# Two-layer fp32 kernel: one h-tile split moved ahead of a Gelu, row transposes grouped in twos, and a reordered tail

## What is computed

```python
# layer 0: an MLP, whose last 128 output columns use an expert chosen per batch
h = gelu(x @ fc1_w.T + fc1_b)                     # 512 -> 2048
x = x + concat(h @ fc2_w.T + fc2_b,               # 2048 -> 384
               h @ experts_w[e].T + experts_b[e]) # 2048 -> 128
# layer 1: masked pooling
s = tanh(x @ W1 + b1) @ v                         # one score for each token
p = softmax(where(mask, s, -1e30))                # mask: l <= j, l >= j or l != j, by batch
x = x + (p @ x) / count_of_mask
```

## Time and profile before

| | us |
|---|---|
| median of 3 runs | 774.71 |
| lowest and highest | 774.32 and 776.2 |
| the profiled execution's own time | 774.91 |
| its span, first to last instruction | 773.1 |
| PE busy in the span | 760.9 |

### The profile page before, as it was taken

The page is one execution under the profiler, slowest core; times in us unless marked ns, Lnnn a source line. Parts: engine busy times, 40 slices in busy tenths (PEclk is TensorE's granted clock), DMA queues, the critical chain, the costliest instruction groups (busy, mean ns, idle before and its releaser), DMA issues.

```text
span 773.1 us, 11505 instructions
## 1 busy us (share of the span) xinstructions
PE 760.9 (98%) x3465; PEld 621.8 (80%) x3465; DVE 403.2 (52%) x701; ACT 387.4 (50%) x669; POOL 131.8 (17%) x199
## 2 busy tenths in 40 slices
PE   8999999999999999999999999999999999999996
PEld 6788888888888888888888888888888888888875
DVE  6955666573445332754545433286355533246767
ACT  6856665453546533544446633445354662344543
POOL 3273230400011121320001022040000102204001
PEclk9999999999999999999999999999999999999998
DMA  6999997877874558877776566886787566697732
GB/s 218 297 338 325 311 348 260 273 227 234 246 205 150 177 190 285 261 218 234 214 231 207 150 202 214 277 257 180 244 260 205 171 189 205 214 287 216 212 113 109
DMA packets 130715, 176.93 MB, mean 229 GB/s; under 512 B 10064, under 2 KB 97632, under 8 KB 130656
## 3 DMA queue, kind: packets, MB, share of 16 engines
q1 hardware_dynamic: 130496, 176.20, 72.7%
q0 software_dynamic: 160, 0.01, 0.1%
HBM read 136.33 MB, written 39.85 MB: 228 GB/s over the span
## 4 chain that ended last, share of the span: by engine, by line
PE 93%; DVE 3%; ACT 1%; DMA 1%; issue 1%; SPq 0%; DVEq 0%
PE y L778 15%; PE y L780 15%; PE y L779 15%; PE hA L778 7%; PE hA L779 7%; PE hA L780 7%; PE hF L778 5%; PE hF L780 5%; PE hF L779 5%; PE j L871 2%; PE j L848 1%; PE j L850 1%; PE j L847 1%; PE j L778 1%; PE j L779 1%; PE j L780 1%
## 5 line engine op out<-in xcount | busy, mean ns | idle before, releaser
L778 PE MATMUL y<-hs,w2c 128*128 128x512 f32 x512 | 201.9, 394 | 0.6 <-DMA w2c<-exs 0.4
L780 PE MATMUL y<-hs,w2c 128*128 128x512 f32 x512 | 199.6, 390 | 0.0
L779 PE MATMUL y<-hs,w2c 128*128 128x512 f32 x512 | 199.3, 389 | 0.0
L778 PEld LDWEIGHTS y<-hs,w2c 128*128 128x128 f32 x512 | 96.1, 188 | 22.8 <-DVE hs L1300 1.9
L780 PEld LDWEIGHTS y<-hs,w2c 128*128 128x128 f32 x512 | 96.1, 188 | 20.5
L779 PEld LDWEIGHTS y<-hs,w2c 128*128 128x128 f32 x512 | 96.2, 188 | 19.3
L778 PE MATMUL hA<-xch,w1c 128*128 128x512 f32 x252 | 99.4, 394 | 2.2 <-DVE xcl L1300 1.7
L780 PE MATMUL hA<-xch,w1c 128*128 128x512 f32 x252 | 98.2, 390 | 0.0
L779 PE MATMUL hA<-xcl,w1c 128*128 128x512 f32 x252 | 98.2, 390 | 0.0
L1048 ACT ACTIVATE hst<-hst,bcol 128x512 f32<-128x512 f32 x62 | 43.9, 721 | 85.2 <-DVE hst L1500 85.2
L1300 DVE TENSOR_TENSOR hs<-gb,hs 128x512 fp32r<-128x512 f32 x64 | 43.5, 716 | 64.4 <-ACT hs L994 64.4
(11 more groups left out here) (284 smaller groups left out, 1110.2 us busy)
## 6 DMA issues: line engine op xcount, KB each, us to landing
w2c<-w2s SPq DMA_DIRECT2D x114, 384.0 KB, 3.6
w1c<-w1s SPq DMA_DIRECT2D x24, 768.0 KB, 4.6
w2c<-exs SPq DMA_DIRECT2D x114, 128.0 KB, 4.0
w1c<-w1s SPq DMA_DIRECT2D x48, 256.0 KB, 3.8
w1c<-w1s SPq DMA_DIRECT2D x24, 512.0 KB, 4.0
x1T<-in_x SPq DMA_DIRECT2D x32, 256.0 KB, 5.8
w1s<-w1c SPq DMA_DIRECT2D x8, 768.0 KB, 4.1
w2s<-w2c SPq DMA_DIRECT2D x16, 384.0 KB, 4.3
```

Of the source, the lines that this page charges most:

```text
L778: nc.tensor.matmul(ps, ah, bh, start=first, stop=False, skip_group_check=onto)
L779: nc.tensor.matmul(ps, ah, bl, start=False, stop=False, skip_group_check=onto)
L780: return nc.tensor.matmul(ps, al, bh, start=False, stop=last, skip_group_check=onto)
```

## The change

There are four edits.

1. In the last pair of a batch, ACT makes the high part of h tile 14 before it waits for the second Gelu (order 4) and not after it.
2. In the stages, the row transposes `xn` 0 and 1 both follow unit 21 (u = 7), and `xn` 2 and 3 both follow u = 9. Before they stood at u = 7, 8, 9 and 10. The difference `xs` 5 moves from u = 9 to u = 10.
3. In the tail, the 8 pieces of units 30 and 31 come in the order of `LAST_UNITS`: two pieces of unit 30 come before the first of unit 31.
4. In the tail, the scans, the exponentials (now `expG` for two of them and `expO` for the other two), `total`, `den` and `rd` come earlier. `own_chunk` 0 to 3 stand ahead of `rd`, and 4 to 7 in one block behind the first four `pool`. Low part 1 of W stands on DVE behind `pool` 3.

```diff
-          6: [("attn",)], 7: [("xn", 0)], 8: [("xn", 1)], 9: [("xn", 2)], 10: [("xn", 3)], 11: [("score",)]}
+          6: [("attn",)], 7: [("xn", 0), ("xn", 1)], 9: [("xn", 2), ("xn", 3)], 11: [("score",)]}
...
+LAST_UNITS = [(-2, 0), (-2, 1), (-1, 0), (-1, 1), (-2, 2), (-1, 2), (-2, 3), (-1, 3)]
...
-    ("expPW", 0), ("sums",), ("scan",), ("expPW", 1), ("total",)] + [("pool", c) for c in range(BC)] + [
-    ("den",), ("rd", 0, CH)] + [("pool", c) for c in range(BC, CH)]
-
-OWN_BEFORE = {("total",): range(BC), ("pool", 0): [4], ("rd", 0, CH): [5], ("pool", 6): [6], ("pool", 7): [7]}
+    ("expPW", 0), ("scan",), ("sums",), ("total",), ("expPW", 1), ("den",), ("rd", 0, CH)] + [("pool", c) for c in range(CH)]
+
+OWN_BEFORE = {("rd", 0, CH): range(BC), ("pool", BC): range(BC, CH)}
...
-    ("full", 2), ("expP", 0), ("expW", 0), ("hiP", 0), ("hiW", 0), ("full", 3), ("expP", 1), ("hiP", 1), ("sums",), ("expM",),
-    ("expW", 1), ("hiW", 1)]
+    ("full", 2), ("expG",), ("expP", 0), ("hiP", 0), ("expW", 0), ("hiW", 0), ("full", 3), ("expO",), ("sums",),
+    ("expP", 1), ("hiP", 1), ("expW", 1), ("hiW", 1)]
...
-FULL_BEFORE = {("bc", 0): 1, ("bc", 1): 2, ("total",): 4}
+FULL_BEFORE = {("bc", 0): 1, ("bc", 1): 2, ("total",): 3, ("rd", 0, CH): 4}
...
-                gate(pool, den_exp, b * NEXP + (6 - NEXP))
+                gate(pool, den_exp, b * NEXP + (5 - NEXP))
                 gate(pool, den_scan, b * NSCAN + (2 - NSCAN))
                 nc.gpsimd.tensor_tensor(short_of(FG), short_of(FG), short_of(FS), ALU.mult).then_inc(den_in, 1)
                 gate(pool, den_in, b * NIN + (5 - NIN))
+                gate(pool, den_exp, b * NEXP + (6 - NEXP))
...
-                    for oc in range(OC):
-                        for n in (-2, -1):
-                            fc2(kind, b, n, oc)
+                    for n, oc in LAST_UNITS:
+                        fc2(kind, b, n, oc)
...
                 gelu(b, p, 3)
+                if p == PAIRS - 1:
+
+                    split_h(b, 2 * p)
                 gelu(b, p, 4)
...
-                split_h(b, 2 * p)
+                if p < PAIRS - 1:
+                    split_h(b, 2 * p)
                 split_h(b, 2 * p + 1)
```

More of the change, by code:

```diff
@@ L86 @@
 POST_U = {1: [("ysum", oc) for oc in range(OC)], 2: [("x1", 0)], 3: [("x1", 1)], 4: [("x1", 2)], 5: [("x1", 3)],
[L87 removed]
+          6: [("attn",)], 7: [("xn", 0), ("xn", 1)], 9: [("xn", 2), ("xn", 3)], 11: [("score",)]}
 PREP_U = {0: [("xc", 0), ("xs", 0)], 2: [("xc", 1), ("xs", 1)], 3: [("xc", 2)], 4: [("xc", 3), ("xs", 2)],
[L90 to L91 removed]
+          5: [("xc", 4), ("xc", 5)], 6: [("xs", 3)], 7: [("xc", 6)], 8: [("xc", 7), ("xs", 4)], 9: [("xc", 8)],
+          10: [("xc", 9), ("xs", 5)], 11: [("xc", 10), ("xs", 6)], 12: [("xc", 11), ("xc", 12)], 13: [("xs", 7)], 14: [("xc", 13)]}
 EX_P = [(0, 1), (1, 0), (1, 2), (2, 1)]
@@ L97 @@
 X_LOADS = {5: ((0, 1), 3, 2), 7: ((3,), 4, 3), 8: ((2,), 6, 3)}
+LAST_UNITS = [(-2, 0), (-2, 1), (-1, 0), (-1, 1), (-2, 2), (-1, 2), (-2, 3), (-1, 3)]
 TAIL_ORDER = [("ysum", oc) for oc in range(OC)] + [("x1", oc) for oc in range(OC)] + [
     ("xn", 0), ("xn", 1), ("attn",), ("xn", 2), ("xn", 3), ("score",), ("stats",), ("expE",), ("mT",), ("bc", 0), ("bc", 1),
-    ("expPW", 0), ("sums",), ("scan",), ("expPW", 1), ("total",)] + [("pool", c) for c in range(BC)] + [
-    ("den",), ("rd", 0, CH)] + [("pool", c) for c in range(BC, CH)]
-OWN_BEFORE = {("total",): range(BC), ("pool", 0): [4], ("rd", 0, CH): [5], ("pool", 6): [6], ("pool", 7): [7]}
+    ("expPW", 0), ("scan",), ("sums",), ("total",), ("expPW", 1), ("den",), ("rd", 0, CH)] + [("pool", c) for c in range(CH)]
+OWN_BEFORE = {("rd", 0, CH): range(BC), ("pool", BC): range(BC, CH)}
 TAIL_ACT = [("x1", oc) for oc in range(OC)] + [
     ("xn", 0), ("xn", 1), ("attn",), ("xn", 2), ("xn", 3), ("full", 0), ("full", 1), ("expE",), ("expS",), ("expF",), ("expD",),
-    ("full", 2), ("expP", 0), ("expW", 0), ("hiP", 0), ("hiW", 0), ("full", 3), ("expP", 1), ("hiP", 1), ("sums",), ("expM",),
-    ("expW", 1), ("hiW", 1)]
+    ("full", 2), ("expG",), ("expP", 0), ("hiP", 0), ("expW", 0), ("hiW", 0), ("full", 3), ("expO",), ("sums",),
+    ("expP", 1), ("hiP", 1), ("expW", 1), ("hiW", 1)]
 TAIL_DVE = [("ysum", 0), ("ysum", 1), ("x1", 0), ("ysum", 2), ("x1", 1), ("ysum", 3), ("x1", 2), ("x1", 3), ("xn", 0),
-            ("xn", 1), ("score",), ("stats",), ("mT",), ("xn", 2), ("expE",), ("bc", 0), ("xn", 3), ("bc", 1), ("loP", 0), ("loW", 0),
-            ("scan",), ("loP", 1), ("sums",), ("total",), ("loW", 1), ("den",), ("rd", 0, CH)] + [("pool", c) for c in range(CH)]
-FULL_BEFORE = {("bc", 0): 1, ("bc", 1): 2, ("total",): 4}
+            ("xn", 1), ("score",), ("stats",), ("mT",), ("xn", 2), ("expE",), ("bc", 0), ("xn", 3), ("scan",), ("loP", 0), ("loW", 0),
+            ("bc", 1), ("total",), ("sums",), ("den",), ("loP", 1), ("rd", 0, CH)] + [("pool", c) for c in range(BC)] + [
+            ("loW", 1)] + [("pool", c) for c in range(BC, CH)]
+FULL_BEFORE = {("bc", 0): 1, ("bc", 1): 2, ("total",): 3, ("rd", 0, CH): 4}
 def body(kind):
@@ L1136, in task_part @@
                 elif task[0] == "expM":
-                    exps_M(b)
+                    exp_runs(b)
+                    exp_own(b)
+                elif task[0] == "expG":
+                    exp_runs(b)
+                elif task[0] == "expO":
+                    exp_own(b)
                 elif task[0] == "expPW":
@@ L1165, in exp_decay, with exp_runs @@
                 nc.scalar.activation(decay[:, :, :], decay[:, :, :], ACT.Exp).then_inc(den_exp, 1)
-            def exps_M(b):
+            def exp_runs(b):
                 act.wait_ge(den_in, b * NIN + (3 - NIN))
@@ L1171, in exps_M, with exp_own @@
                 nc.scalar.activation(FG[:, P + 3:2 * P + 3], FG[:, P + 3:2 * P + 3], ACT.Exp, bias=TM[:, NP_:NP_ + 1]).then_inc(den_exp, 1)
+            def exp_own(b):
                 act.wait_ge(den_in, b * NIN + (4 - NIN))
@@ L1335, in task_part @@
                     dve.wait_ge(xres_in[oc], T * 16 + 16)
-                    done = (HC - 2) * OC + 2 * oc + 2 if kind == "tail" else (HC - 1) * OC + oc + 1
+                    done = (HC - 2) * OC + LAST_UNITS.index((-1, oc)) + 1 if kind == "tail" else (HC - 1) * OC + oc + 1
                     dve.wait_ge(fc2_done, T * (HC * OC) + done)
```

## The result

The first measurement, seven executions of each kernel, gave 772.54 us for the changed kernel (771.02 to 773.4) and 775.24 for the kernel before (773.31 to 776.6). The medians are 2.7 us apart. The ratio on record, by which measurements are compared here, is 0.997 with a 95% interval of 0.9956 to 0.9984: about 2.3 us faster, 1.2 to 3.4. The mean of the three is 0.33%, 2.6 us. The forecast was 771.3 with a range of 769.9 to 773.0. So its sign and its range held. Its size, a ratio of 0.9956, lies at the very end of the interval: the sum of 3.44 us is too large. The median of 772.54 is also above the narrower range of 770.6 to 772.1 that the forecast had for itself, and beside the times of two rivals, 772.4 (the tail gives all back) and 772.6 (the wait for tile 14 is only replaced).

What follows compares the result with a forecast made beforehand. PE was taken as the bound, busy 760.9 of 773.1 us. Savings of 1.28 + 0.4 + 0.65 + 1.11 = 3.44 us from 774.91 gave 771.47, and 0.2 to the median 771.3; range 769.9 to 773.0, 8 in 10.

Steps and rivals of the forecast that it cites:

- the tail gives all back: Tail: `rd` or the second half comes over a microsecond later than counted, giving 772.4 us; 14 in 100.
- the wait for tile 14 is only replaced: End of the last pair: PE then stops for tile 15 or an `xc`, giving 772.6 us; 6 in 100.
- Edit 1, 1.28 us: End of each batch's last pair: four waits for `hs` vanish, 0.26 + 3 x 0.34 = 1.28 us.
- Edit 2, 0.4 us: Stages with transposes: one burst in place of two saves 0.05 to 0.06 us, eight times, 0.4 us.
- The rival of a falling clock: Stages: the clock falls after doubled transposes, 1.7 us per burst, 784.9 us if all eight; 2 in 100.
- Edit 3, 0.65 us: First matmul of unit 31 in the tail: 0.65 of its 0.69 us wait for weights is saved.
- The landing is the uncertain part: Unit 31's weights land at 738.70, 0.2 us before PE comes; a landing 0.7 later leaves no gain.
- Edit 4, 1.11 us: Tail: the first `pool` starts 2.41 us earlier, part is given back, the last `pool` gains 1.11 us.
- The give-back: Tail: DVE waits for PE's last four matmuls after low part 1 of W; `pool` 4 starts at 766.45.
- So `den` ends near 761.2, 0.5 early: Tail, DVE: `den` is ready 0.5 us before PE comes to `rd` at 761.70.
- The clock in the tail: Between 752.60 and 756.40 the granted clock averages 0.55; a 1.7 us loss on the path, kept.
- the clock stays high: Tail: no low stretch of the granted clock, giving 769.6 us; 5 in 100.

Runs made afterwards that it cites:

- the three: Three measurements of the whole changed kernel against the kernel before: ratios 0.997, 0.9958 and 0.9973.
- `den` first: The changed kernel with `den` ahead of the low part of `Bs` on DVE: 772.62 us, ratio to the kernel before 0.9961.
- edit 4's own profile: The kernel before with only the tail's new order: 774.98 us against 775.59, ratio 0.999.
- second profile of the changed kernel: The whole change measured again, unaltered, against the kernel before: 772.23 us, ratio 0.9958.
- profiles of edits 2 and 3: The kernel before with only the regrouped transposes (775.29 us, ratio 0.9993), and with only the new order of units 30 and 31 (774.81 us, ratio 0.999).
- filling matmuls: Four more matmuls with unused product on PE ahead of `stats`: 771.91 us in the changed kernel, 774.57 in the kernel before.
- last profile of the changed kernel: The whole change measured a third time, unaltered, against the kernel before: 772.28 us, ratio 0.9973.
- The four edits measured alone: Each edit by itself on the kernel before, in order: 774.25, 775.29, 774.81 and 774.98 us against 775.59.
- either place of the low part: Low part 1 of W on DVE behind `pool` 3, as in the changed kernel, or behind `pool` 2: 771.32 us, ratio 0.995 for the latter.

## Why the prediction was right, and where its sum was off

**Edit 1, 1.28 us.** The mechanism is right: the four waits are gone. The size is right in part by luck. Three batches gave 0.36 and not 0.34 each, because I had left the slow distances after a wait out of the sum. The first batch gave 0.04 and not 0.26, since a wait at unit 20 took most of it back: 1.12 us in all, 1.36 if that wait is absent. The rival "the wait for tile 14 is only replaced" was thought of with PE stopping for tile 15 or an `xc`; what came, in one batch, was a wait in the stages.

**Edit 2, 0.4 us.** Right in sign and nearly in size: 0.48. The recovery, which was the only unknown, was not what I took it for: a fixed 0.05 after each burst. In the profile before, the stages with four transposes take 3.21, 3.19 and 3.21 us (713.27, 716.48 and 719.67 to 722.88), which leaves 0.05, 0.03 and 0.05. Over one burst of eight and its two stages 6.33 us pass, where my terms give 2 x 2.72 + 0.87 + 0.05 = 6.36: 0.02 is left. Why it differs was not tested. The rival of a falling clock did not come; in the same window the clock is 1.00:

```profile
711.91:718.24 6.33, 6.33 (x34) 5.33 (x33) 4.10 (x7) 4.13 (x8) 0.00 (x0) 1.00 0.44 129
```

By the rule of the Trainium skill that I weighed there ("TensorE: Matmul & The Clock Gate", Part 4, PE-mode transpose: transposes do not count as activity as matmuls do), it could have. At this length the trace does not show it.

**Edit 3, 0.65 us.** The mechanism was right and the term mis-sized: 0.3 in the mean of profiles, 0.47 in the first one (5.67 to 5.22). "The landing is the uncertain part", I wrote, but I took it from one execution, and it was one of the two longest waits of five.

**Edit 4, 1.11 us.** This is the step that failed in part. Its sign of being wrong, PE waiting ahead of `rd` for `den`, is in the new profile. The `rd` matmul comes 4.55 us after the last of `sums` (756.11 to 760.66) where I had 3.1, and `pool` 3 ends after 8.25 where I had 6.6; a good part of both is that `sums` itself was over sooner, at the high clock. The give-back is 1.45 us, 0.16 more than my 1.29 (764.28, where `pool` 4 would have been due, to 765.73). What was wrong is the sentence "So `den` ends near 761.2, 0.5 early": I took PE's arrival at `rd` as what decides, with DVE half a microsecond ahead. In fact DVE decides in all nine profiles of the new tail, at 9.2 us after the first broadcast (9.4 with `den` first), where I had 8.97 (762.52 - 753.55). Two things made it so. DVE's list is longer than counted: the low part 0 of W took 1.04 us, not 0.68, in the time of POOL's product of FG and FS, which took 1.13 and not 0.74. So `den` ended 8.06 us after the broadcast, where I had 7.65. Both show the longer time in edit 4's own profile too. In four of the nine profiles that low part starts 0.26 later and takes 0.78 or 0.79; it ends at the same 4.88 us after the broadcast. And PE's arrival depends on the clock: I used a `sums` partly at the low clock, which put PE at `rd` 8.15 us after the broadcast; with the high clock of the new profile it was there after 7.21. In the second profile of the changed kernel, where a part of `sums` ran at the low clock, PE's wait for `den` was only 0.13 us.

Between the same marks the gain is 15.99 - 15.27 = 0.72 us for the clock as it was before, and 0.34 for a high clock (15.61 to 15.27). So my 1.11 was 0.39 too high: 0.22 at the first `pool` and about 0.16 in the give-back. For a low clock all through `sums`, as in the profiles of edits 2 and 3, no profile of the new tail exists. An estimate: the last matmul of `sums` started 5.92 us after the broadcast there (edit 2), and in the new tail PE reaches `rd` 3.20 us after that matmul (756.02 to 759.22 in the profile with `den` first), so at 9.1 and not at 8.2. Then PE decides, the last `pool` comes about 0.75 later than 15.27, and the gain is about 0.9 us, not the full 1.7 between 17.00 and 15.27 that I had expected further up.

The Trainium skill ("SBUF — State Buffer", Who interferes with whom) says that a DVE operation with two SBUF inputs and a GpSimd operation that reads SBUF exclude each other for a whole instruction. The two long durations (1.04 and 1.13 us) agree with that; no run took one of the two away, so this cause is argued and not shown.

**The clock in the tail.** I kept it as a fixed loss of 1.7 us on the path. It was 0.6 in that profile, by the old tail with the filling matmuls (25.87 against 25.24): a part of the slow time passed beside DVE's list. So the rival "the clock stays high" promised too much with its 769.6. Where the loss falls differs by execution: on `sums`, where the new tail didn't feel it in the cases seen (`sums` of up to 4.4 us from first start to last), or on the chain ahead of the broadcast, where both tails do. In the first profile after, it cost about 1.1 us there. The broadcast on DVE came 10.73 us after the first attention matmul, where it comes after 9.6 us with a high clock (741.24 to 750.87 in the last profile of the changed kernel). That is why this profile shows nothing of edit 4.

**The sum.** For the clock as it was in the profile before, the terms measured in traces are 1.12 + 0.48 + 0.3 + 0.72 = 2.6 us, in place of 3.44. Over the states of clock and loads they are 1.1 to 1.36, 0.48, 0.3 and 0.3 to 0.9: 2.2 to 3.0 us. The four edits measured alone give 1.4 + 0.5 + 0.8 + 0.8 = 3.5 us by their ratios, each uncertain by about 1, and the whole change 2.3, 3.3 and 2.1. So nothing is lost between the edits beyond what can be measured. That the start of the kernel took 0.09 us more in the profile after (144.96 against 144.87 to the first attention matmul) is within its spread: it was 144.3 to 147.2 in the profiles here.

## What to carry to other kernels

Where executions differ by more than an edit is worth, measure the edit between two marks of the trace that enclose it; these repeated to 0.02 to 0.06 us in all but two batches, where the times needed ten executions for 1 us. Look through the whole stretch for what the gain turns into: here a wait of 0.2 us at a load, 17 us later, took most of it back in one batch. When a wait of the busiest engine is removed, add up the list of the next engine from a fixed mark before believing the new start time: here a margin of 0.5 us became a wait of 1.0, 0.4 by the list and the rest by a faster clock of the engine that waits. An operation that starts a round trip over another engine belongs one operation earlier than the last moment.

## What the runs showed of the hardware

- After a burst of four transposes or a wait, the next eight or nine matmuls of 128x512 stand 0.231 us apart (714.17 to 716.25 and 688.98 to 690.83 in the profile before), not 0.227. A burst of four is followed by 0.03 to 0.05 us of this, a burst of eight by 0.01 to 0.02 (6.33 us for the burst and its 24 matmuls).
- The low stretch of the granted clock in the tail came in nine of ten profiles without filling matmuls, at changing places, and in none of four with four more matmuls in a pause of 1.1 us.
- DVE's low part of 32x512 took 0.68 us alone. Beside a POOL operation that took 1.13 or 1.14 in place of 0.74 it took 1.04 to 1.06 in five profiles, and 0.78 or 0.79 in the four in which it started 0.26 later.
- One of the eight issues on SP that send the rows out took 1.46 us in one execution, and one took 0.67, 0.75 and 0.83 in three others, where the rest took 0.33 to 0.46. Such an issue came with either place of the low part. The cause stays open.
- The 128 KB of expert weights for unit 31 took 5.2 to 6.1 us to land in the four profiles whose chain shows it, where such loads have a median of 3.8 to 4.1 by profile.
